# Causal and full attention: the first unit's key and query stacks projected in place by repeated weight columns

## The reference, cut to what matters

```python
# layer 1, causal (B, S, D = 2, 1024, 256; 16 heads of 16 columns)
q = split_heads(x @ Wq + bq); k = split_heads(x @ Wk + bk); v = split_heads(x @ Wv + bv)
scores = jnp.einsum('bhqd,bhkd->bhqk', q, k) / math.sqrt(hd)
scores = jnp.where(causal[None, None], scores, -10000.0)
ctx = jnp.einsum('bhqk,bhkd->bhqd', jax.nn.softmax(scores, axis=-1), v)
x = _layernorm(x + ctx_rows @ Wo + bo)

# layer 2, full: one weight for all heads, no bias in q, k, v, no mask
q = jnp.einsum('bshd,ed->bshe', xh, Wq)          # k and v likewise
attn = jax.nn.softmax(jnp.einsum('bqhd,bkhd->bhqk', q, k) / jnp.sqrt(e), axis=-1)
x = _layernorm(x + out_rows @ W_out.T + b_out)
```

## Time and profile before

| what | us |
|---|---|
| median of 3 runs (2862.24 to 2866.62) | 2865.63 |
| the profiled execution's own time | 2864.44 |
| its span | 2862.7 |
| causal stage, first projection to the first `st_ps` matmul | 340.2 to 400.2 |
| full stage, first projection to the first `st_ps` matmul | 1237.5 to 1294.95 |

### The profile page before, as it was taken

How to read it: one execution, slowest core, us unless ns; L and a number is a source line. 1 busy time by engine, 2 the same in 40 slices (tenths; PEclk the granted TensorE clock), 3 DMA queues, 4 the chain that set the end, 5 groups by cost and what they waited for, 6 DMA issues and landing times. The chain is left out here.

```text
span 2862.7 us, 43236 instructions
## 1 busy us (share of the span) xinstructions
PE 2440.5 (85%) x16008; PEld 1610.0 (56%) x16008; DVE 1434.2 (50%) x3136; ACT 1198.3 (42%) x2119; POOL 626.4 (22%) x799
## 2 busy tenths in 40 slices
PE   2389799998987999769999988589799798499996
PEld 2377654444434799744444443366666443379996
DVE  6625367784554222257888945565344444621113
ACT  6433335555333111126777762311444332433444
POOL 5100112221100133221101001121044411044551
PEclk8679979998988999959999999688999897699998
DMA  5100122220003299721121100032000100379996
GB/s 191 47 0 1 32 46 38 41 45 19 6 2 122 70 325 334 275 50 23 32 38 24 24 9 2 12 119 71 23 2 3 41 2 2 118 248 327 351 353 235
DMA packets 82425, 264.74 MB, mean 92 GB/s; under 512 B 22766, under 2 KB 42758, under 8 KB 65952
## 3 DMA queue, kind: packets, MB, share of 16 engines
q1 hardware_dynamic: 67560, 229.12, 25.2%
q0 software_dynamic: 14144, 31.81, 3.2%
q10 hardware_dynamic: 512, 1.05, 0.2%
HBM read 212.09 MB, written 23.94 MB: 82 GB/s over the span
## 5 line engine op out<-in xcount | busy, mean ns | idle before, releaser
L1347 DVE TENSOR_REDUCE cmax<-ring 128x1 f32<-128x512 f32 (+3 forms) x896 | 514.8, 625 | 149.4 <-PE ring L1213 80.4
L1332 ACT ACTIVATE prob<-st_ps 128x1024 f32<-128x1024 f32 x448 | 413.5, 933 | 171.6 <-PE st_ps L1205 169.4
L2722 PE MATMUL A<-xbT,w 128*128 128x128 f32 x2512 | 301.6, 276 | 1.2 <-DMA w<-L1f_W_dram 0.9
L2722 PEld LDWEIGHTS A<-xbT,w 128*128 128x128 f32 x2512 | 291.6, 193 | 1.7 <-DMA w<-L1f_W_dram 1.1
L1213 PE MATMUL ring<-kst,qst 48*128 48x512 f32 (+3 forms) x896 | 238.2, 426 | 43.4 <-DMA qst<-parts 23.1
L1253 PE MATMUL acc<-prob,v 128*32 128x256 f32 (+2 forms) x3200 | 260.9, 399 | 1.2 <-POOL prob L1145 0.7
L2730 PE MATMUL C<-w,hid 128*128 128x256 f32 x944 | 223.1, 379 | 0.0
L1205 PE MATMUL st_ps<-qst,kst 64*128 64x512 f32 (+3 forms) x896 | 217.5, 482 | 3.5 <-DMA qst<-crow 1.8
L2967 DVE COPY yb<-C 128x256 f32<-128x256 f32 x118 | 50.1, 424 | 284.4 <-PE C L2730 278.0
L1213 PEld LDWEIGHTS ring<-kst,qst 48*128 48x128 f32 x896 | 138.0, 197 | 91.7 <-DVE cmax L1347 52.4
L2642 POOL DMA_INDIRECT y_rows_dram<-yb,dst x118 | 116.5, 987 | 324.7 <-DVE yb L2967 321.5
(11 more groups left out here) (434 smaller groups left out, 4304.7 us busy)
## 6 DMA issues: line engine op xcount, KB each, us to landing
w<-L3f_W_dram SPq DMA_DIRECT2D x79, 1026.0 KB
w<-L1f_W_dram SPq DMA_DIRECT2D x39, 1536.0 KB
kst<-parts SPq DMA_DIRECT2D x192, 64.0 KB, 2.4
qst<-parts SPq DMA_DIRECT2D x168, 64.0 KB, 2.4
gate<-L2f_gates_dram SPq DMA_DIRECT2D x6, 1536.0 KB, 8.7
room<-y_rows_dram SPq DMA_DIRECT2D x8, 1024.0 KB, 10.8
raw<-L2f_W_dram SPq DMA_DIRECT2D x12, 384.0 KB, 9.3
x_rows_dram<-x SPq DMA_DIRECT2D x2, 2048.0 KB, 7.9
```

What stands on the lines that cost most here:

```text
L1332: act.activation(prob[:, step % PROBS, 2 * p:2 * p + 2, 0:n], st_ps[:, p, :, 0:n], ACT.Exp, scale=scale)\
L1347: dve.tensor_reduce(cmax[:, a, t:t + 1, k0 // CH], spot(key)[:, 0:k1 - k0], AX.X, ALU.max)\
L2722: mm = pe.matmul(A[:, j % 2 * 2 + a, f * TB:(f + 1) * TB], up_w(w[:, j % WB], a, k, f), xbT[:, j % 2, k, :], start=(k == 0), stop=(k == KT ...
```

## The change

For unit 0 alone the stacks are no longer copied. Before the first projection, VectorE and ScalarE write a weight tile `ws` in which each head's 16 key (query) columns stand three times (line 1464 and 1362 of the changed kernel), GpSimd zeroes the fourth block. One projection with it (`project_stack`, two matmuls of 128x256) gives a quarter of the tokens in the layout of the stack. ScalarE writes its signed high part to `half_hi` (`first_parts`), with a scale of +1 or -1 by partition; VectorE computes value × mask + `half_hi` into the stack (`stack`), where the mask `low` is 1 on the rows of the low part. In causal a VectorE instruction before it adds the bias (`whole`). There are 16 such items: keys and queries, two pairs of heads, four quarters.

The 8 splits of units 0 and 1 stay, for unit 1, but move from ahead of the lead into it; so do ten of the 16 stack items. The table `opening` sets this. Unit 1's copies are now issued as 12 key copies once 4 splits are done and 12 query copies once 8 are done. The clearing of `qst` slot 0 goes; the memsets of `kst` move from VectorE to GpSimd and lose slot 0.

```diff
+    if kind == "causal":
+        opening = [stack_of("keys", 0) + stack_of("keys", 1) + stack_of("queries", 1), stack_of("queries", 0), splits[0:2], splits[2:4],
+                   stack_of("queries", 2), splits[4:6], stack_of("queries", 3), splits[6:8], stack_of("keys", 2) + stack_of("keys", 3),
+                   [("values", 0, x) for x in (0, 1)], [("values", 0, x) for x in (2, 3)]]
+    else:
+        opening = [stack_of("keys", 0) + stack_of("keys", 1) + stack_of("queries", 0), stack_of("queries", 1), stack_of("keys", 2),
+                   stack_of("keys", 3), splits[0:2], splits[2:4], stack_of("queries", 2), splits[4:6], splits[6:8],
+                   stack_of("queries", 3) + [("values", 0, 0)], [("values", 0, x) for x in (1, 2, 3)]]
...
-        items = []
+        items = list(opening[c + 1]) if c < LEAD else []
...
-    for item in splits[0:8]:
-        enter(item, 0)
+    for item in opening[0]:
+        enter(item, 1)
...
+                    sp.wait_ge(s.split, 8 * (g // 2) + 4)
+                    for h in range(HU):
+                        copy(sp, g, h, 1, KEY_ROWS, stacked[g % SLOTS])
                     sp.wait_ge(s.split, 8 * (g // 2 + 1))
                     for h in range(HU):
-                        copy(sp, g, h, 1, KEY_ROWS, stacked[g % SLOTS])
                         copy(sp, g, h, 0, QUERY_ROWS, stacked[g % SLOTS])
...
+                def project_stack(of, x):
+                    which, hp = of
+                    key = ("stack", of, x)
+                    room(key)
+                    for kt in range(KT):
+                        at = (which * KT + kt) * HU + 2 * hp
+                        mm = pe.matmul(spot(key)[:, 0:QUART], ws[:, at:at + 2, :].rearrange("p h n -> p (h n)"),
+                                       env.xT[:, kt, x * QUART:(x + 1) * QUART], start=(kt == 0), stop=(kt == KT - 1), skip_group_check=True)
+                    mm.then_inc(s.dve_filled, 1)
...
                     if k and x == 0:
                         for g in (2 * k - 2, 2 * k - 1):
-                            act.wait_ge(*stacks_done(g))
-                        if k == 1:
-                            act.wait_ge(s.opened, 16 * 2 * HU)
-                            act.wait_ge(s.opened_low, 16 * HU)
+                            if g:
+                                act.wait_ge(*stacks_done(g))
...
+                def first_parts(of, x):
...
+                    act.wait_ge(s.dve_filled, filled(key))
+                    if n >= 4:
+                        act.wait_ge(*freed_of(stack_items[n - 4]))
+                    act.activation(half_hi[:, n % 4, :], spot(key)[:, 0:QUART], ACT.Identity, bias=signed[:, which, hp:hp + 1],
+                                   scale=env.sign[:, which:which + 1]).then_inc(s.hi_first, 1)
...
+                def stack(of, x):
...
+                    dve.wait_ge(s.hi_first, n + 1)
+                    if loaded_biases:
+                        if n:
+                            dve.wait_ge(*freed_of(stack_items[n - 1]))
+                        dve.tensor_scalar(whole[:, :], value, env.sb[:, which, hp:hp + 1], None, ALU.add).then_inc(s.summed, 1)
+                        dve.wait_ge(s.summed, n + 1)
+                        value = whole[:, :]
+                    to = qst if which else kst
+                    dve.scalar_tensor_tensor(out=to[:, 0, hp, x * QUART:(x + 1) * QUART], in0=value, scalar=env.low[:, which:which + 1],
+                                             in1=half_hi[:, n % 4, :].bitcast(F32), op0=ALU.mult, op1=ALU.add).then_inc(s.dve_freed, 1)
```

More of the change, by code:

```diff
@@ L939, in stacked_attention, with stack_of @@
     values_at = (3, 5, 6, 7) if kind == "causal" else (2, 3, 4, 5)
+    def stack_of(what, x):
+        return [("stack", (int(what == "queries"), hp), x) for hp in range(2)]
+    if kind == "causal":
[6 more added lines that the diff above has]
+                   stack_of("queries", 3) + [("values", 0, 0)], [("values", 0, x) for x in (1, 2, 3)]]
     def projections_due(c):
@@ L975, in stacked_attention @@
         for item in projections_due(c):
-            enter(item, int(item[0] == "values" and biased))
+            enter(item, int(item[0] == "stack" or item[0] == "values" and biased))
     def masked_sides(step):
@@ L1039, in freed_of, with stack_need @@
                 return freed(entries[key][0])
+            stack_items = [key for some in opening for key in some if key[0] == "stack"]
+            def stack_need(c):
+                t, k0, k1, _ = chunks[c][0]
+                keys = [key for x in range(k0 // QUART, (k1 - 1) // QUART + 1) for key in stack_of("keys", x)]
+                return s.dve_freed, max(freed_of(key)[1] for key in keys + stack_of("queries", t * P // QUART))
             def copy(eng, g, h, keys, parts_of_rows, done):
@@ L1112, in splits_due @@
                     for item in projections_due(c):
-                        if item[0] != "values":
+                        if item[0] in ("keys", "queries"):
                             split(item)
+                pool.memset(ws[:, :, 3 * HD:], 0.0).then_inc(s.padded, 1)
                 if not loaded_biases:
                     pool.memset(bias[:, :, :], 0.0).then_inc(s.bias_ready, 16)
[L1118 to L1124, removed]
                 pool.memset(cmax[:, :, :, :], -3e38).then_inc(s.max_cleared, 1)
@@ L1229, in extras @@
                     for what, g, x in projections_due(c):
-                        if what == "values":
+                        if what == "stack":
+                            project_stack(g, x)
+                        elif what == "values":
                             project_values(g, x)
@@ L1259, in _ @@
                 pe.wait_ge(env.w_ready, w_count)
-                for item in splits[0:8]:
-                    project(*item)
+                pe.wait_ge(s.padded, 1)
+                pe.wait_ge(s.copied, 2 * KT)
+                for _, of, x in opening[0]:
+                    project_stack(of, x)
                 for c in range(LEAD):
```

99 lines of the change are left out of this document (67 added, 32 removed).

## The result

| | before | after |
|---|---|---|
| median of 4 and 4 runs, us | 2866.12 (2862.24 to 2873.99) | 2900.08 (2894.42 to 2902.4) |
| the profiled execution, its own time | 2864.44 | 2894.42 |
| its span, mean granted clock | 2862.7, 0.896 | 2892.6, 0.901 |

The ratio of after to before is 1.0112, interval 1.0086 to 1.0138: slower by 34 us in the medians, where 24 were predicted. The direction and the place are as forecast. The size came out of another term than the one on which the forecast spent most words, as the experiments show.

What follows compares the result with a forecast made beforehand. The prediction took whatever delays TensorE, up to each stage's first st_ps, as the bound. Causal +14.1, full +5.9 and short idles +4 made 24: 2889 us, 0.8% slower; own range 2878 to 2898, 8-in-10 range 2866 to 2908.

Steps and rivals of the forecast that it cites:

- The added wait: In c6 (causal) and c7 (full), query copies issue behind the eighth split; TensorE stands 10.8 and 5.7 us, plus 2.85 clock loss each.
- The rival that the wait doesn't bind: In the lead, SP or GpSimd is ready earlier or copies land in time: +1.7 us, 2867; chance 0.11.
- the faster one: Rival in the lead: VectorE bounds the pieces, added items cost little, the wait does not bind: -14 us, 2852; chance 0.08.
- SP's issues: Twelve query copies behind the eighth split: the last issue begins 7.1 us later and lands 2.4 after that.
- The lead after: Lead with 18 items more, at clock 1.0: causal first st_ps at 400.6 without the wait, full c9 ending at 1293.5.
- short idles, +4: Short TensorE gaps in the new lead drop the clock: half the time, 2 to 3 us lost each, +4 us.
- The rival in which the clock stays low (2906): Clock stays at 0.50 through both leads, each added item costs 1.72 us: about +40, 2906; chance 0.11.
- the hole: TensorE's idle of some 12 us ahead of the first piece drops the lead's clock to 0.50; without it 1.0 expected.
- Items: Price of each further split or stack item in the lead: 0.88 us at full clock, 1.72 at half.
- The opening: Weight copies 1.3 us before the first projection (0.6 to 1.8); first piece 10.6 us earlier in causal, 10.8 in full.
- The rule's estimate: VectorE and GpSimd exclude each other on a shared port pair: at most one memset in each stage, some 3.6 us.
- The sum: Causal +14.1, full +5.9, short idles +4: 24 us, giving 2889 us, 0.8% slower.

Runs made afterwards that it cites:

- e1: The changed kernel with key copies counted on semaphores of their own, so a key split no longer waits for query copies: 2876.19 us, ratio 1.0055 to before.
- e4: The kernel before with 24 unread matmuls filling the idle of 12 us ahead of the first piece: 2863.14 us, ratio 0.999 to before.
- e5: The kernel before with the idle filled by 24 unread matmuls and one unread matmul behind each lead piece: 2917.47 us, ratio 1.0163 to before.
- e6: The changed kernel with the eight splits of units 0 and 1 projected ahead of the lead, behind six stack items: 2878.93 us, ratio 1.005 to before.
- e3: The changed kernel with query stack items in the causal lead moved a chunk ahead of the chunk needing them: 2894.08 us, ratio 1.0117 to before.
- e9: e8 with each of the ten stack items of both leads projected twice, 20 projections more: 2877.90 us, ratio 1.0048 to before.
- e8: The changed kernel with the edits of e1 and e2 together: 2873.94 us, ratio 1.0033 to before.
- e2: The changed kernel with GpSimd's memsets of cmax, qst, kst and v held behind weight copies and signed biases: 2891.07 us, ratio 1.0111 to before.

## Why the prediction was right, and where its sizes were not

**The added wait: right in kind and place.** The forecast said that ScalarE at the third split of c6 would wait for twelve query copies issued behind the eighth split, that two pieces would still go out, and that the third would stand for 10.8 us in causal and 5.7 in full. The trace has two pieces and 9.48 and 3.62. With the clock's 2.85 behind each, the forecast priced the wait at 22.2 us; e1, which takes this wait away, got back 22.5 in the front parts. That the two agree so closely is partly luck: the idles were 13.1 us, and the half clock behind them lasted 4.0 and 3.4 us, not 5.7, which makes some 17 us in all by this trace (an estimate from these rows); where the rest came from is open. The rival that the wait doesn't bind is out, and so is the faster one.

**SP's issues: right.** Forecast 7.1 us to the last of twelve and 2.4 to land from the earlier trace rows, 9.5 in all; measured 407.13 - 399.66 = 7.47 for all twelve and 1.8 from their end until ScalarE goes on, 9.3.

**The step that failed: "The lead after", by its clock of 1.0.** I wrote "there is no 12 us hole, so I expect 1.0 at its start" and worked out all chunks at full-clock prices. The start was at 1.0; in causal the clock fell 1.1 us behind the first piece. Taking the wait's idle out of the front parts, the pieces of the sum are:

| us | causal forecast | causal | full forecast | full |
|---|---|---|---|---|
| stage start to first piece | 11.2 | 12.8 | 10.6 | 11.5 |
| lead without the idle, the 2.85 included | 52.1 | 65.1 | 48.3 | 54.8 |
| idle of the wait | 10.8 | 9.5 | 5.7 | 3.6 |

The lead is 13 and 6.5 us too short in the forecast; the term "short idles, +4" was meant for it and covers a fifth. The rival in which the clock stays low (2906) named the right quantity. What happened lies between: 0.63 and 0.75 up to the wait, where it had 0.50 and the forecast 1.0. In causal all 13 us lie ahead of the wait: 44.9 us from the first piece to the end of c6, forecast 31.8, and behind the wait 19.5, forecast 19.6. A clock of 0.63 over 44.9 us costs at most 0.37 of them, 16.6 us, if all of it were TensorE's (an estimate), so it is large enough; but no run kept the clock at 1.0 through such a lead, so that all 13 are the clock's is not shown.

The cause I gave for the low clock before, the hole, is refuted: e4 has no hole and falls, e5 hardly idles and falls. What makes it fall in these stretches is open. What the rows of the leads show is that it stands at 1.00 while TensorE does projections or the fill alone (e6's eight splits, 352.6 to 360.3, and e4's fill) and falls 1.1 to 10.3 us behind the start of the lead's pieces (after, e4, e5). In the causal lead of after, outside the wait, it falls four times (355.8, 379.7, 393.4, 420.7), each time 1.1 to 2.5 us behind the end of a TensorE idle of 1.15 to 2.29 us; in the full lead it also falls where no idle within 5 us ahead was over 0.52 us (1287.7, 1308.2, 1318.4). So the term for short idles may have had the right cause and too small a size; e3 and e5 do not settle it.

**Items: TensorE's part a little dear, the whole too cheap.** I charged 0.88 us for each further item. e9 says 0.54 for TensorE's part of one more projection. But in e8, where nothing waits for the copies, the leads are 23.1 and 17.4 us longer than before (61.3 and 53.5 against 38.2 and 36.1) for 18 items, 1.3 and 1.0 each, with the clock at 0.75 and 0.81, so that they cost more than their price at full clock. The added VectorE and ScalarE instructions take 0.48 and 0.56 us in the trace, where I took 0.42 and 0.47.

**The opening: above its upper bound.** I took 1.3 us for the weight copies and gave 1.8 as the upper end "if they queue behind something". They took 2.49 to the first projection, and the opening saved 9.1 and 9.9 us where 10.6 and 10.8 were forecast. The row on which I had ruled the conflict out was two memsets at once, which is another pair of instructions. Measured, it is the rule's side that holds: in after the two copies last 2.30 us beside a GpSimd memset, in e2 0.55 alone, and even `signed`, two columns wide, 1.85 against 0.35. The Trainium skill (SBUF — State Buffer, "SBUF: two separate sides") has it as an exclusive lock on a shared port pair, held for a whole instruction; this case's traces agree for copies and the two-column scaling, at 1.7 us to the first projection, and show nothing of it for two memsets. The rule's estimate in the forecast, up to 3.6 us in both stages together, is the 3.4 that e2 found.

**The sum.** Front parts: forecast +14.1 and +7.1 and 4 of dips, 25.2; measured 39.8. Behind the front parts the difference of these two traces ran the other way by 11.7 us (3.3 and 8.4), of which 1.25 were forecast and the rest is unexplained. The medians say +34. So the result lies 11 us above the forecast and inside its wide range, and that it is no further off is luck: the front parts alone were 14.6 us dearer than forecast. The forecast's own range ended at 2898. Its sentence that behind the lead every queue keeps its order is not so either: the key copies of the later pairs are issued after four splits too, and TensorE's idles there are 1.92 and 2.21 us where they were 2.69 and 2.63.

**What stays of the change without the wait.** The change still costs 10 to 15 us without its wait (e1, e6, e8). Its gain in the opening, 9.6 to 12.3 us per stage in e1 and e8 and some 4 in e6, which keeps the splits there, is in each of them; what the added items cost in the lead is more than that.

## What to carry to other kernels

When work is moved from an opening into the loop behind it, look first at which later instruction waits for the batch that the moved item issues: here a writer waited for all 24 copies of a batch, though it needed only the twelve that were issued 24 us before the others. Counting the two halves of the batch on two semaphores gave back some 21 us in the changed kernel, and in the old one, with the key copies put first, 0.38% (0.19 to 0.56), which made it faster than both. And price work that is moved at the clock of the place where it goes, which may be the lower one even when nothing idles there.

## What the runs showed of the hardware

- The granted clock fell under a TensorE busy for 10.25 of 10.30 us, and stayed at 0.50 for 36.3 us in which its modelled busy time has no gap (e5). Unread matmuls did not hold it up and cost 0.8 us each.
- A VectorE copy and a scaling of two columns waited for whole GpSimd memsets: 2.30 against 0.55 us and 1.85 against 0.35 (after, e2). A stack write of 128x256 inside a memset did not, at 0.48 us (after, 347.77).
- Twelve copies of 64 KB between SBUF tensors, issued one behind another by SP, take 7.47 to 7.61 us of its queue, 0.63 each, for queries as for keys. Of the 9.3 us from their first issue until ScalarE goes on (after), the issuing was 7.5.
